# Probabilities times values in three fp32r passes, with a regrouped mix and a prologue that takes the second half early

## What is computed

```python
    x = x + attn(layernorm(x), ...)           # first part: cumulative sums, products of rank 64
    # second part, h = layernorm(x)
    normed = rmsnorm(h) * norm_w
    v_pool = concat([normed, ctx])            # values and keys: 1024 tokens and 77 context rows
    q = normed @ q_w.T;  k = v_pool @ k_w.T
    logits = (q @ k.T) * 256 ** -0.5          # masked so that a token sees itself and what is before it
    attn = softmax(logits)
    h_tilde = attn @ v_pool                   # probabilities times values
    alpha = sigmoid(h @ gate_w.T + gate_b)
    x = x + (1 - alpha) * h + alpha * h_tilde # the mix
    x = x + ffn(layernorm(x), ...)            # third part, operands in 4-bit blocks
```

## Time and profile before

| | |
|---|---|
| median of 3 runs | 591.12 us (588.67, 591.12, 591.13) |
| the profiled execution | 588.64 us, of which 586.9 us span |
| TensorE busy | 540.8 us (92%), mean granted clock 0.994 |
| VectorE busy | 482.6 us (82%) |
| ScalarE busy | 314.3 us (54%) |
| GpSimd busy | 295.4 us (50%) |
| prologue | 0 to about 59 us, the first logits of batch 0 |
| batches 0 to 3 | about 77 us from the first logits of a batch to those of the next, the last to about 351 us |
| feed-forward loop | from about 352 us to the end |

### The profile page before, as it was taken

How to read it: one execution, slowest core, us unless ns; L and a number is a source line. 1 busy time by engine, 2 the same in 40 slices (tenths; PEclk the granted TensorE clock), 3 DMA queues, 4 the chain that set the end, 5 groups by cost and what they waited for, 6 DMA issues and landing times.

```text
span 586.9 us, 10801 instructions
## 1 busy us (share of the span) xinstructions
PE 540.8 (92%) x3156; PEld 473.3 (81%) x3156; DVE 482.6 (82%) x1251; ACT 314.3 (54%) x710; POOL 295.4 (50%) x389
## 2 busy tenths in 40 slices
PE   4969899998999999999988987799999999999995
PEld 4756787887878888878877865699999999999995
DVE  3467789886799867887678968899999999999985
ACT  3234643525544436354444356677777777777652
POOL 4021912618117082361436515877777777777740
PEclk9989899999999999999999999999999999999999
DMA  7620400000000000000000000000000000000001
GB/s 216 194 74 0 150 2 0 2 1 0 0 0 0 0 0 2 0 2 2 0 1 2 0 1 1 2 18 18 18 19 26 18 18 18 18 18 21 25 20 36
DMA packets 16125, 13.78 MB, mean 23 GB/s; under 512 B 3884, under 2 KB 15840, under 8 KB 16096
## 3 DMA queue, kind: packets, MB, share of 16 engines
q1 hardware_dynamic: 16095, 13.43, 7.3%
HBM read 9.23 MB, written 4.19 MB: 23 GB/s over the span
## 4 chain that ended last, share of the span: by engine, by line
PE 70%; DVE 17%; issue 6%; ACT 4%; POOL 2%; DVEq 1%; ACTq 0%; POOLq 0%
PE ps L857 16%; PE ps L858 16%; PE ps L859 16%; PE ps L1052 7%; PE ps L1195 3%; DVE dmix L1365 2%; PE ps L972 2%; PE ps L973 2%; PE ps L1040 2%; DVE X L1369 1%; DVE mx L1350 1%; PE ps L1050 1%; ACT xn_sums L608 1%; DVE parts L1270 1%; PE ps L944 1%
## 5 line engine op out<-in xcount | busy, mean ns | idle before, releaser
L857 PE MATMUL ps<-keys_h,nT_h 128*128 128x256 f32 (+6 forms) x304 | 94.4, 310 | 3.5 <-DVE keys_l L1270 1.8
L858 PE MATMUL ps<-keys_l,nT_h 128*128 128x256 f32 (+6 forms) x304 | 92.1, 303 | 0.0
L859 PE MATMUL ps<-keys_h,nT_l 128*128 128x256 f32 (+6 forms) x304 | 91.8, 302 | 0.0
L857 PE MATMUL ps<-parts,xq_parts 128*128 128x512 f32 (+1 forms) x192 | 77.5, 404 | 7.2 <-DVE xq_parts L1456 7.2
L647 ACT ACTIVATE prob<-ps,nbias 128x205 f32<-128x205 f32 (+7 forms) x32 | 25.7, 805 | 93.2 <-DVE nbias L1352 93.2
L859 PE MATMUL ps<-parts,xq_parts 128*128 128x512 f32 (+1 forms) x192 | 72.0, 375 | 0.0
L858 PE MATMUL ps<-parts,xq_parts 128*128 128x512 f32 (+1 forms) x192 | 71.9, 374 | 0.0
L1052 PE MATMUL ps<-V,probT 128*128 128x256 f32 x288 | 67.4, 379 | 0.0
L857 PEld LDWEIGHTS ps<-keys_h,nT_h 128*128 128x128 f32 x304 | 57.2, 188 | 7.7 <-issue 2.2
L1052 PEld LDWEIGHTS ps<-V,probT 128*128 128x128 f32 x288 | 54.6, 189 | 7.7
L858 PEld LDWEIGHTS ps<-keys_l,nT_h 128*128 128x128 f32 x304 | 57.3, 188 | 3.1
(11 more groups left out here) (205 smaller groups left out, 1506.8 us busy)
## 6 DMA issues: line engine op xcount, KB each, us to landing
X<-in_x_dram SPq DMA_DIRECT2D x8, 512.0 KB, 5.9
out_dram<-X SPq DMA_DIRECT2D x32, 128.0 KB, 1.7
early<-in_L_ffn_w_down_dram SPq DMA_DIRECT2D x1, 704.0 KB, 6.5
early<-in_L_ffn_w_gate_dram SPq DMA_DIRECT2D x1, 640.0 KB, 4.3
early<-in_L_ffn_w_up_dram SPq DMA_DIRECT2D x1, 640.0 KB, 5.1
ctx_rows<-in_ctx_dram SPq DMA_DIRECT2D x1, 308.0 KB
early<-in_L_attn_Winv_dram SPq DMA_DIRECT2D x1, 256.0 KB, 3.9
early<-in_L_attn_WQ_dram SPq DMA_DIRECT2D x1, 256.0 KB, 4.8
```

The costliest lines, as they stand in the source:

```text
L857: mm(o, wh, mh, start=start, stop=False, **kw)
L858: mm(o, wh, ml, start=False, stop=False, **kw)
L859: return mm(o, wl, mh, start=False, stop=stop, **kw)
```

## The change

- The product of probabilities and values goes through `mm_parts`. For that the probabilities have a low part (`probT_l`, made by a new function `turn_low` on VectorE), and the values a high part (`V_h`, made on ScalarE by `values_high`) and a low part (`V_l`, made on GpSimd by `values_low`); GpSimd's product with the norm weights is now written over `nrm`. The context block stays in float32.
- The mix is regrouped. ScalarE turns the tanh into the sigmoid by a second activation (0.5 t + 0.5), GpSimd forms (1 - alpha) h as X + h - alpha h (`base_tiles`, two tiles at a time), and VectorE does two operations instead of three. The statistics of a batch are copied once, not once a tile, and the maximum is negated where it is taken; the scale of the logits is folded into the weights.
- Four tiles of the layer input `hid` are kept, not eight, so `hid_half(b + 1, 0)` on ScalarE and its sum on GpSimd move to the end of a batch.
- In the prologue, the second half of batch 0 is normalised, transposed and projected right behind the first, into other banks and other SBUF, and gate_w is turned later.
- Some tiles lie elsewhere: `scanA` shares the room of `xn`, and the feed-forward's `hmag`, `ht` and `hq_wide` lie in `raw`.

```diff
+    def values_low(b, h):                              # GpSimd
+        pool.wait_ge(s_V_h, q + 1)
+        for i in range(h * HALF, (h + 1) * HALF):
+            g.tensor_tensor(V_l[:, i, :], nrm[:, i, :], V_h.bitcast(F32)[:, i, :], ALU.subtract).then_inc(s_V, 1)
+    def base_tiles(b, tiles):                          # GpSimd
+        pool.wait_ge(s_th, b * TPB + (tiles[-1] + 1))
+        for i in tiles:
+            g.tensor_tensor(hid[:, i % HALF, :], hid[:, i % HALF, :], th[:, i % HALF, :], ALU.mult).then_inc(s_gated, 1)
...
+        for i in tiles:
+            g.tensor_tensor(X[:, b * TPB + i, :], X[:, b * TPB + i, :], hid[:, i % HALF, :],
+                            ALU.subtract).then_inc(s_base, 1)
     def batch(b, more, ahead=False):                   # GpSimd
-        base_half(b, 0)
+        values_low(b, 0)
+        base_tiles(b, (0, 1))
+        base_tiles(b, (2, 3))
         values_half(b, 1)
-        base_half(b, 1)
+        sum_half(b, 1)
+        values_low(b, 1)
...
+            sum_half(b + 1, 0)
             values_half(b + 1, 0)
+    def values_high(b, h):                             # ScalarE
+        act.wait_ge(s_values, b * 2 + (h + 1))
+        act.wait_ge(s_pv, START + b * TPB)
+        a.activation(V_h[:, c, :], nrm[:, c, :], ACT.Copy).then_inc(s_V_h, 1)
     def turn_tile(b, i):                               # TensorE
             if k >= 2:
-                pe.wait_ge(s_probT, START + b * CPB + (k - 1))
+                pe.wait_ge(s_probT_l, START + b * CPB + (k - 1))
     def pv_tile(b, i):                                 # TensorE
         for m in range(1, i + 2):
-            last = mm(ps[:, 5, 0:D], probT[:, i % 2, m, :], V[:, m - 1, :], start=False, stop=(m == i + 1))
+            last = mm_parts(ps[:, 5, 0:D], (probT_h[:, i % 2, m - 1, :], probT_l[:, i % 2, m - 1, :]),
+                            (V_h[:, m - 1, :], V_l[:, m - 1, :]), start=False, stop=(m == i + 1))
+    def turn_low(b, i):                                # VectorE
+        for c, blocks in enumerate(chunks[i]):
+            ve.wait_ge(s_probT, START + b * CPB + (k + 1))
...
+            low(probT_l[:, i % 2, m0 - 1:m1 - 1, :], ps[...], probT_h[...]).then_inc(s_probT_l, 1)
     def mix_tile(b, i):                                # VectorE
-        v.scalar_tensor_tensor(dmix[:, 0, :], ps[:, 5, 0:D], rinv[:, i:i + 1], hid[:, i, :], ALU.mult,
-                               ALU.subtract).then_inc(s_mix1, 1)
+        v.scalar_tensor_tensor(dmix[:, 0, :], ps[:, 5, 0:D], rinv[:, i:i + 1], th[:, i % HALF, :], ALU.mult,
+                               ALU.mult).then_inc(s_mix1, 1)
-        v.scalar_tensor_tensor(dmix[:, 1, :], th[:, i % HALF, :], 1.0, dmix[:, 0, :], ALU.add,
-                               ALU.mult).then_inc(s_mix2, 1)
-        v.scalar_tensor_tensor(X[:, n, :], dmix[:, 1, :], 0.5, X[:, n, :], ALU.mult, ALU.add).then_inc(s_x2, 1)
+        v.tensor_tensor(X[:, n, :], dmix[:, 0, :], X[:, n, :], ALU.add).then_inc(s_x2, 1)
     def batch(b, more, ahead=False):                   # VectorE
+            if i == TPB:
+                turn_low(b, TPB - 1)
...
+            if 1 <= i < TPB:
+                turn_low(b, i - 1)
             if i >= 2:
                 mix_tile(b, i - 2)
     # TensorE, prologue
     turn_xn(0, 0, 0)
+    make_proj_w()
     spread_inv_count()
-    make_proj_w()
...
-    proj_tiles(0, (0, 1))
-    make_out_w()
-    proj_tiles(0, (2,))
-    make_att_w()
-    proj_tiles(0, (3,))
+    proj_tiles(0, (0, 1), (6, 7, 4, 5))
+    turn_xn(0, 1, 1, xn1, 0)
+    proj_tiles(0, (2, 3), (6, 7, 4, 5))
+    make_out_w()
+    turn_ctx()
+    make_att_w()
     y_half(0, 0)
-    turn_ctx()
-    turn_xn(0, 1, 1)
-    proj_tiles(1, range(4))
+    proj_tiles(1, (0, 1), (0, 1, 4, 5), (xnT1_h, xnT1_l))
+    turn_weight(2, gw)
+    proj_tiles(1, (2, 3), (0, 1, 4, 5), (xnT1_h, xnT1_l))
+    make_ctx_keys()
     turn_nrm(0, 0); turn_nrm(0, 1)
-    make_ctx_keys()
     y_half(0, 1)
```

More of the change, by code:

```diff
@@ L260, in decoder_layer @@
         s_V = sem("V")
+        s_values = sem("values")
+        s_V_h = sem("V_high")
+        s_sum = sem("sum")
+        s_gated = sem("gated")
         s_base = sem("base")
@@ L754, in _ @@
             a.activation(proj_h[:, :, 5 * R:6 * R], xt[:], ACT.Copy)
[L755 to L757 removed]
+            act.wait_ge(s_rstd1, 2)
+            carry()
+            for i in range(HALF):
+                last = a.activation(xn1[:, i, :], X[:, HALF + i, :], ACT.Identity,
+                                    bias=shift1[:, HALF + i:HALF + i + 1], scale=rstd1[:, HALF + i:HALF + i + 1])
+            last.then_inc(s_xn, 1)
             act.wait_ge(prep_mm, 2)
@@ L1551, in _ @@
             bi_half(0, 0, 0)
-            tri_half(0, 0)
+            tri_half(0, 0, 4)
+            for j in range(2):
+                c = slice(j * 2 * P, (j + 1) * 2 * P)
+                ve.wait_ge(s_xnT_h, 2 + (j + 1))
+                low(xnT1_l[:, :, c], ps[:, j, :].rearrange("p (k n) -> p k n", k=KD), xnT1_h[:, :, c]).then_inc(s_xnT_l, 1)
             ve.wait_ge(prep_mm, 6)
```

257 lines of the change are left out of this document (145 added, 112 removed).

## The result

The changed kernel took 602.53 us (median of 4 runs, 600.1 to 603.34), the kernel before 591.12 us in the same runs: a ratio of 1.019, interval 1.0149 to 1.0235. It is slower by 1.9%; I had forecast 597 us, inside a range of 579 to 605. The profiled execution has a span of 600.6 us where the kernel before had 586.9, so 13.7 us are to be found.

The account below looks back on a forecast made before the run. TensorE and VectorE were taken as tied to each other in a batch. Prologue -6.4, heads +8.4, middles -1.5 and tails +8.0 gave +8.5 us on the profiled 588.64: 597 us, range 579 to 605.

Parts of the forecast that it names:

- The product: Probabilities times values on TensorE: three passes at 0.354 us a block replace float32 at 0.431, saving 2.8 us a batch.
- The tails: Iterations 7 to 8: third chunk of tile 7 waits for low parts, delaying y; +3.6, +3.6, +1.7, -0.9, together +8.0 us.
- y takes 3.5 us: Step at a batch's end: y, starting behind the third chunk's transpose, was taken to last 3.5 us.
- The heads: Iterations 0 to 3: sum, values and V_h delay tile 1's exponential; +4.1, +1.3, +1.3, +1.7, together +8.4 us.
- The middles: Iterations 3 to 7: VectorE's low parts and lighter mix cancel; 0, but -1.5 us in batch 3.
- The prologue: Before the first logits: TensorE's projections run without gaps, first logits at 52.7 in place of 59.15; -6.4 us.
- TensorE decides: Rival: VectorE is ahead in the tail, so heads and tails cost nothing; 571 us, chance 0.10.
- only part of the waits: Rival: waits eat just the product's gain while the prologue's gain stays; 582 us, chance 0.18.
- waits at half: Rival: waits at heads and tails cost half of what was computed; 589 us, no change, chance 0.14.
- no prologue gain: Rival: the prologue's second half still waits for GpSimd or a bank, giving 2 us, not 6.4; 601 us, chance 0.08.
- The estimate of 593 us: Side estimate by the VectorE-GpSimd lock: L1365 no longer loses 6.7 us, additions to X lose 2.4 more; 593.
- GpSimd decides: Rival: GpSimd's larger work brings sum and values 3 us later at each head; 605 us, chance 0.10.

Follow-up runs that it names:

- tail_early: Changed kernel with VectorE's low parts of tile 7's first two chunks moved ahead of the mix of tile 5; 594.17 us, ratio 1.0090 to the kernel before.
- head_values: Changed kernel with GpSimd multiplying the next batch's first-half values before adding its sum; 593.33 us, ratio 1.0073 to the kernel before.
- one_pass: Changed kernel with only the high-parts pass of three in the values' product, other engines unchanged; 597.40 us, ratio 1.0140 to the kernel before.
- tail_filled: Changed kernel with idle TensorE matmuls into a free bank during the wait ahead of tile 7's third chunk; 596.27 us, ratio 1.0130 to the kernel before.
- product_f32: Changed kernel with the values' product back in float32, no low parts of probabilities, V_h and V_l still made; 581.87 us, ratio 0.9881 to the kernel before.
- product_undone: Changed kernel with the float32 product back and V_h, V_l and probabilities' low parts all removed; 572.49 us, ratio 0.9722 to the kernel before.
- no_low: Changed kernel with three passes but no low parts of probabilities, high parts used twice; 578.49 us, ratio 0.9814 to the kernel before.
- undone_late: Changed kernel with the float32 product fully restored and the prologue's second half back behind the context keys; 580.96 us, ratio 0.9851 to the kernel before.
- prologue_late: Changed kernel with the prologue's second-half transposes and projections back behind the context keys; 609.23 us, ratio 1.0329 to the kernel before.

## Why the prediction was right, and where it was not

**Right in class and mechanism.** The sign, the wait for probT_l at L1100 (3.5 us in batches 0 and 1, 1.5 in batch 2, as written), V_h held by sum and values, and the tie of the earlier trace rows, in which TensorE's saving is worth next to nothing: tail_early, head_values and one_pass show each. Batches 0 and 1 took 84.2 and 82.5 us, inside my 81 to 85; batch 2, with 79.0, did not. By stretches the forecast was 5.2 us short: tails 4.6, heads 2.6 and loop 1.2 too low, prologue 2.0 and middles 1.2 too high. Without these last two the time would have been just outside the range, so that it lies inside is in part luck.

**The product (-2.8 us a batch).** The size was right as TensorE's time, and next to nothing of it shows in the changed kernel. The Trainium skill ("FP8 and Floating Point Precision", section "TensorE Precision Notes") gives true FP32 as four passes through the array; the trace has 0.431 us for a float32 block, where four passes of 0.118 would be 0.472, and 0.354 for three passes, so it agrees only roughly. The 0.077 us a block that are saved are little beside the low parts.

**The tails (+8.0, measured +12.6).** The failed step is "y takes 3.5 us". It takes 5.9 us (204.5 to 210.4), since the engine comes out of a 3.5 us wait at 1.2 GHz. tail_filled measures the term that was missing at 3.0, 2.4 and 1.7 us. The wait was sized well: counted from exp(7), y starts 3.2, 3.5 and 1.4 us later in tail_filled than in the kernel before, where I had +3.6, +3.6 and +1.7. Its tails are only +2.3, +2.6 and +0.4, since 1 us comes back behind y: in batch 1, from y to ScalarE's norm 11.1 us in place of 11.5, and from there to exp(0) 4.0 in place of 4.6. Most of that is the shorter product of tiles 6 and 7, since with the float32 product (product_f32) these stretches take 11.5 and 4.4; the part of tile 7 I had counted in the heads. In batch 3 -0.9 became +0.3: the wait ahead of the third chunk is no longer than before (1.63 beside 1.67 us), but the clock is at 1.2 GHz behind it from 356 to 359 us, which costs 1.7. The clock was in my text only for the prologue. The Trainium skill ("TensorE: Matmul & The Clock Gate", section "HAM oscillation — how this bites in real kernels") describes waits for a DMA between bursts of matmuls, after which each burst starts at the lower clock. The windows above show the same behind a wait for VectorE, and by it the term would have been in the sum.

**The heads (+8.4, measured +11.0 to exp(3)).** At the logits of tile 3, where my steps ended, it was right: counted from exp(0), 14.3 in place of 10.7 us in batch 0 (+3.6; forecast +4.1), and 13.7 in place of 12.5 in batch 1 (+1.2; forecast +1.3). Part of that agreement is luck. In batch 0 TensorE ran at 1.2 GHz from 52 to 59 us, which was not in my steps; in batch 1, counted from ScalarE's norm, where the steps began, it is only +0.6 (17.8 us in place of 17.1). The rest is VectorE's wait of 1.56 us behind exp(2), which I had seen, counted in the middle, and taken as given back. Head and middle together are +8.3, forecast +6.9. Taken apart by the runs: V_h with its values costs 3.9, 0.8, 1.3 and 1.3 us (product_f32 less product_undone; in batch 0 a fall of the clock is in it), the low parts 1.7, 2.2, 2.1 and 0.8 (changed less product_f32).

**The middles (-1.5, measured -2.7) and the cancelling of low parts and mix.** I let the lighter mix and the low parts cancel and put both at 0. They do not. In the middle of batch 1 the low parts cost nothing (36.5 us with them, and 36.5 without them in no_low), and the lighter mix alone gives 1.4 (36.8 in place of 38.2); so batches 0 to 2 came out at -4.1, not 0. In batch 3 I had -1.5 and it was +1.5: there the low parts of the probabilities cost 1.3 us (33.1, and 31.9 in no_low and 31.8 in product_f32), and V_h and V_l another 1.8 (30.0 in product_undone). Over the whole kernel undone_late shows the mix to be worth 9 us of its own, and product_undone the whole product with its parts to cost 28 us.

**The prologue (-6.4, measured -8.2 to -8.4).** Handed on. The first projections were 1 us and the first logits 1.7 us ahead of what I had stepped through.

**The loop (0, measured +1.2).** The clock is 0.90 between 580 and 590 us and 0.93 in the next 10 us of this trace, 1.7 us lost in all; in the kernel before it is 1.00 from 560 to 580 and 0.95 from there to its end.

**The rivals.** "TensorE decides" fell to one_pass, "only part of the waits" and "waits at half" to the waits as measured, "no prologue gain" to prologue_late. The estimate of 593 us did not come, though its terms did: the additions to X took 20.2 us in place of 17.0 (+3.2, estimate +2.4), and L1365 with its 6.7 us of hindrance is gone. That the middles of batches 0 to 2 came out 4 us lower than in my sum may be this; no run takes it apart. "GpSimd decides" named a time close to the result (605) for a reason that did not hold: in batch 1 V_h came 1.1 us later than in my steps, about what the norm was late already. That its first two pieces stood in the wrong order was part of the loss. Its total work was not: head_values has all of it and V_h hardly waits, and product_undone has GpSimd busy 43.9 us in a batch and is the fastest.

In one line: prologue -8, mix and gates -9, product with all its parts +28, each from ratios that are good to some 5 us. The change is two good edits and one bad one.

## What to carry to other kernels

- Splitting the float32 product into three passes saved TensorE 18% of it here (0.354 in place of 0.431 us a block), and has to be paid by whoever makes the low parts. Where an engine order ties TensorE to VectorE, ask first where the low part is waited for, then how long the product is. In a change with several parts, measure each part by itself: here two were worth 17 us and hidden by the third.
- Price a new wait of TensorE of several us with what comes behind it at half the clock. If it cannot be removed, try idle matmuls into a free bank: here they were cheaper than the lower clock (7 us of tails).
